# Unit stores on ScalarE's queue, tiles prepared earlier, transfers in quarters, and VectorE instead of GpSimd for the low parts of the turned tiles

## What is computed

```python
x = x + tanh(g_xattn) * cross_attention(layernorm(x), ctx)   # 16 heads, 128 keys per sequence; there are no text keys
x = x + tanh(g_ffn) * ffn(layernorm(x))
# ffn(h): y = square(relu(h @ up)) @ down + (h @ expert) * sum(top2(h @ gate))
#         layernorm(y) * gamma + beta            up 512x2048, down 2048x512, expert 512x512, gate 512x8
```

## Time and profile before

| | |
|---|---|
| median of 3 runs | 1365.26 us |
| the profiled execution | 1362.92 us, span 1361.1 us |
| TensorE busy | 1277.8 us (94%) |
| VectorE, ScalarE, GpSimd busy | 69%, 56%, 43% |
| mean granted TensorE clock | 0.975 |
| transfers | 276.96 MB, mean 203 GB/s |

### The profile page before, as it was taken

How to read it: one execution, slowest core, us unless ns; L and a number is a source line. 1 busy time by engine, 2 the same in 40 slices (tenths; PEclk the granted TensorE clock), 3 DMA queues, 4 the chain that set the end, 5 groups by cost and what they waited for, 6 DMA issues and landing times.

```text
span 1361.1 us, 26319 instructions
## 1 busy us (share of the span) xinstructions
PE 1277.8 (94%) x9154; PEld 1093.8 (80%) x9154; DVE 943.1 (69%) x1568; ACT 755.8 (56%) x2012; POOL 591.3 (43%) x720
## 2 busy tenths in 40 slices
PE   7999999999899999999999999899999899999993
PEld 5887777777777778788899888799888789887993
DVE  6777777777766876665598665697664896366676
ACT  5877777777666757656455343454343543444440
POOL 3766666666655996463034322043311233111033
PEclk9999999999899999999999999899999999999997
DMA  6588888988878864659675687675677664564861
GB/s 226 140 211 222 220 221 222 231 221 213 218 200 196 205 153 115 228 220 237 233 238 177 225 234 221 202 227 176 239 227 223 220 188 165 193 221 153 230 184 62
DMA packets 335460, 276.96 MB, mean 203 GB/s; under 512 B 233852, under 2 KB 248316, under 8 KB 330239
## 3 DMA queue, kind: packets, MB, share of 16 engines
q1 hardware_dynamic: 297600, 165.79, 45.1%
q10 hardware_dynamic: 37758, 109.85, 24.6%
HBM read 198.79 MB, written 76.81 MB: 202 GB/s over the span
## 4 chain that ended last, share of the span: by engine, by line
PE 49%; DVE 16%; DMA 11%; SPq 7%; issue 6%; POOL 5%; ACT 3%; DVEq 0%; POOLq 0%; ACTq 0%
PE wide L79 15%; PE wide L80 14%; PE wide L81 14%; DMA kd_scratch<-kf 6%; SPq L1649 4%; DVE wo_lo L2006 4%; DMA k_dealt<-kd_scratch 3%; PE wide L418 2%; DMA out_x<-fxy 2%; ACT prob L817 1%; PE wide L406 1%; DVE S L1990 1%; POOL fxy L1447 1%; POOL prob L988 1%; PE wide L1728 1%
## 5 line engine op out<-in xcount | busy, mean ns | idle before, releaser
L817 ACT ACTIVATE prob<-wide,nmx 128x128 f32<-128x128 f32 x512 | 180.7, 396 | 6.0 <-DVE nmx L626 5.9
L988 POOL TENSOR_TENSOR prob<-prob,rr 128x512 f32<-128x512 f32 x128 | 136.1, 1075 | 103.9 <-DVE rr L634 103.9
L79 PE MATMUL wide<-eight,wo_hi 128*128 128x256 f32 x480 | 138.0, 288 | 12.5 <-DVE wo_lo L2006 8.3
L1820 ACT ACTIVATE hid<-wide 128x512 f32<-128x512 f32 x96 | 57.4, 599 | 156.6 <-PE wide L81 156.6
L80 PE MATMUL wide<-eight,wo_hi 128*128 128x256 f32 x480 | 136.4, 284 | 0.0
L81 PE MATMUL wide<-eight,wo_lo 128*128 128x256 f32 x480 | 136.3, 284 | 0.0
L2006 DVE TENSOR_TENSOR wo_lo<-hid,wo_hi 128x512 fp32r<-128x512 f32 x120 | 94.6, 810 | 43.6 <-ACT wo_hi L1820 43.6
L817 ACT ACTIVATION_READ_ACCUMULATOR prob<-wide,nmx 128x1 f32 x512 | 121.1, 236 | 0.0
L1820 ACT ACTIVATE wo_hi<-hid 128x512 fp32r<-128x512 f32 x120 | 74.4, 631 | 79.2 <-PE wide L81 79.2
L79 PE MATMUL wide<-wq_hi,eight 128*128 128x512 f32 x192 | 82.9, 432 | 27.1 <-DVE eight L565 27.1
L79 PEld LDWEIGHTS wide<-eight,wo_hi 128*128 128x128 f32 x480 | 92.8, 193 | 16.3 <-issue 9.4
(11 more groups left out here) (308 smaller groups left out, 3971.0 us busy)
## 6 DMA issues: line engine op xcount, KB each, us to landing
eight<-down_scratch ACTq DMA_DIRECT2D x32, 1024.0 KB, 8.0
wk_hi<-down_scratch ACTq DMA_DIRECT2D x12, 1024.0 KB, 7.8
wk_lo<-down_scratch ACTq DMA_DIRECT2D x12, 1024.0 KB, 7.5
wk_hi<-up_scratch ACTq DMA_DIRECT2D x12, 1024.0 KB, 6.8
eight<-up_scratch ACTq DMA_DIRECT2D x12, 1024.0 KB, 5.8
wk_lo<-up_scratch ACTq DMA_DIRECT2D x12, 768.0 KB, 5.6
eight<-up_scratch ACTq DMA_DIRECT2D x12, 768.0 KB, 7.0
xin<-in_x SPq DMA_DIRECT2D x32, 256.0 KB, 3.4
```

What stands on the lines that cost most here:

```text
L79: eng.matmul(dst, ah, bh, start=first and k == 0, stop=False, skip_group_check=onto)
L817: i = act.activation(prob[par][:, g, h * P:(h + 1) * P], cols(bank[g], h), ACT.Exp, bias=nmx[:, n:n + 1], scale=1.0, accum_out=rs[:, n:n + 1])
L988: pool.tensor_tensor(p, p, r, ALU.mult).then_inc(po_p, 1)
L1820: return act.activation(dst, src, ACT.Copy)
```

## The change

Attention: the unit stores are issued by ScalarE, in two parts, the raw one at the top of a slot, the sums after the slot's exponentials; the eight tiles are loaded one per slot from slot 19, with statistics one slot and normalisation two slots later, the latter on VectorE. Feed-forward: residual loads and output stores go in quarters of 32 rows, `weigh` waits for its own tile's store alone, the last group's stores are shared by SP and ScalarE; `lo_T` moves to VectorE; the order of the partial products is 0, 1, 4, 3, 5, 2, 6, with `sum_4` at later steps and written into `hid[q][:, 2]`; in groups 1 and 2 the statistics of the next tiles come at q 0 and 1 and the layer norm of y at q 4 to 7; in the last group VectorE adds the epsilon to the variance.

```diff
-                    if ff.third_of(s, par) is not None:
-                        ff.unit_store(sp, ff.third_of(s, par))           # in SP's slot
+                    if ff.third_of(s, par) is not None:
+                        ff.unit_store_raw(act, ff.third_of(s, par))      # top of ScalarE's slot
+                    if ff.third_of(s, par) is not None:
+                        ff.unit_store_sums(act, ff.third_of(s, par))     # after exps(s, par, 2) and hi_xT(n + 1)
+    def unit_store_raw(act, uu):
+        at_least(act, ql, uu + 2)
+        for part, src in enumerate((t_hi, t_lo)):
...
+                dst = down_dram[uu][0:3, :, part * H:(part + 1) * H].rearrange("o p n -> p o n")
+                act.dma_start(dst, src[:, 0:3 * H].rearrange("p (o n) -> p o n", n=H)).then_inc(st_q, DMA)
+    def unit_store_sums(act, uu):
+        at_least(act, qd, uu + 2)
...
+                dst = down_dram[uu][3:7, :, part * H:(part + 1) * H].rearrange("o p n -> p o n")
+                act.dma_start(dst, src[:, 3 * H:7 * H].rearrange("p (o n) -> p o n", n=H)).then_inc(st_qs, DMA)
+            TILE_LOADED, TILE_STATS, TILE_DONE, PAIR_SUMS = NB - 13, NB - 12, NB - 11, NB - 6
-                    if ff_pair(s) is not None:
-                        ff.stats(dve, 0, ff_pair(s))
-                        ff.stats(dve, 0, ff_pair(s) + GB)
+                    if ff_turn(s, TILE_DONE, ff.TILES) is not None:
+                        ff.normalise(dve, 0, ff_turn(s, TILE_DONE, ff.TILES))
+                    if ff_turn(s, TILE_STATS, ff.TILES) is not None:
+                        ff.stats(dve, 0, ff_turn(s, TILE_STATS, ff.TILES))
-                            ff.normalise(pool, 0, tile)
-    D_SEQ = (0, 3, 4, 2, 5, 1, 6)
+    D_SEQ = (0, 1, 4, 3, 5, 2, 6)
-    TURN_AT = (9, 10, 12, 13, 14, 15, 16, 17)
-    SUMS_AT = (28, 30, 32, 34)
-    HI_AT = (11, 12, 14, 15, 16, 17, 18, 20, 31, 33, 35, 37, 39, 41, 43, 45)
+    TURN_AT = (9, 11, 12, 14, 15, 17, 18, 20)
+    SUM4_AT = (24, 26, 28, 29, 31, 32, 33, 35)
+    SUMS_AT = (36, 39, 41, 44)
+    HI_AT = (11, 13, 14, 16, 17, 19, 20, 22, 38, 41, 43, 46, 47, 48, 49, 50)
+    Y_AT = {4: (0, 1), 5: (2, 3), 6: (4, 5), 7: (6, 7)}
+    def STATS_AT(g):
+        return 1 if g == 0 else 0
-        eng.dma_start(ff.dealt_rows(out[g * GB + i]), y[i]).then_inc(ff.st_o[i % HB], DMA)
+        for src, dst in ff.quarters(y[i], out[g * GB + i]):
+            eng.dma_start(dst, src).then_inc(ff.st_o[i], DMA)
+    def store_half(eng, i, half):                      # last group: half 0 by SP, half 1 by ScalarE
+        eng.wait_ge(ff.dv_o, GB * LAST + i + 1)
+        for src, dst in ff.quarters(y[i], out[LAST * GB + i])[2 * half:2 * half + 2]:
+            eng.dma_start(dst, src).then_inc(ff.st_o[i], DMA)
-            sp.dma_start(res(g, i), ff.dealt_rows(x2_dram[g * GB + i])).then_inc(ff.ld_r[i % HB], DMA)
+            for dst, src in ff.quarters(res(g, i), x2_dram[g * GB + i]):
+                sp.dma_start(dst, src).then_inc(ff.ld_r[i % HB], DMA)
+        def later_group(g):
+            more = g < LAST
+            if more:
+                load_x(g + 1)
+            for i in range(HB):
+                load_res(g - 1, i)
+            if more:
+                for tile in range(GB - 1):
+                    deal(g + 1, tile)
+            for i in range(HB):
+                store_out(sp, g - 1, i)
+                load_res(g - 1, i + HB)
+                if more and i == 1:
+                    deal(g + 1, GB - 1)
+            for i in range(HB, GB):
+                store_out(sp, g - 1, i)
-            at_least(act, ff.st_o[j % HB], 2 * g * DMA)
+            at_least(act, ff.st_o[j], g * KT * DMA)
-                for tile in {1: range(HB), 2: range(HB, GB)}.get(q, ()):
+                for tile in {STATS_AT(g): range(HB), STATS_AT(g) + 1: range(HB, GB)}.get(q, ()):
                     ff.stats(dve, g + 1, tile)
+                if g < LAST and k - 1 in HI_AT:
+                    ff.lo_T(dve, g + 1, HI_AT.index(k - 1))
+        def variance_last(i):
+            dve.wait_ge(ff.dv_ys, 2 * (GB * LAST + i) + 2)
+            dve.tensor_scalar(ff.yvar[:, i:i + 1], ff.ymv[:, i, 1:2], EPS_LN, None, ALU.add).then_inc(ff.fcst, 1)
-            if g < LAST:
-                for i in range(NT):
-                    ff.lo_T(pool, g + 1, i)
```

More of the change, by code:

```diff
@@ L164, in has, with ff_turn @@
                 return not isinstance(b, int) or 0 <= b < NB
-            def ff_pair(b, after=0):
-                jj = b - (NB - 8) - after if isinstance(b, int) else -1
-                return jj if 0 <= jj < GB else None
+            def ff_turn(b, first, order):
+                n = b - first if isinstance(b, int) else -1
+                return order[n] if 0 <= n < len(order) else None
+            TILE_LOADED, TILE_STATS, TILE_DONE, PAIR_SUMS = NB - 13, NB - 12, NB - 11, NB - 6
             def is_slot(b, n):
@@ L1041, in slot @@
                         inv_std(s + 3)
[L1042 to L1045 removed]
+                    if ff_turn(s, TILE_STATS, ff.TILES) is not None:
+                        ff.inv_std(pool, 0, ff_turn(s, TILE_STATS, ff.TILES))
                     if ff.first_of(s, par) is not None:
@@ L1158, in units_stored, with none_stored @@
     def units_stored(uu):
-        return uu * DMA + (max(uu - 2 * NQ, 0) * DMA if isinstance(uu, int) else 0)
+        return DMA + uu * DMA + (max(uu - 2 * NQ, 0) * DMA if isinstance(uu, int) else 0)
+    def none_stored(sp):
+        sp.sem_inc(st_q, DMA)
+        sp.sem_inc(st_qs, DMA)
     def is_up(uu):
@@ L1206, in unit_parts @@
     def unit_parts(uu, a):
[L1207 to L1211, removed]
+        both = raw[:, 0:D] if is_up(uu) else raw.rearrange("p (n m) -> p n m", n=2)[:, :, 0:H]
+        two = a[:, 0:2 * H] if is_up(uu) else a[:, 0:2 * H].rearrange("p (n m) -> p n m", n=2)
+        return [(two, both), (a[:, 2 * H:3 * H], raw[:, 3 * H:4 * H]),
                 (a[:, 3 * H:5 * H], unit_sum[:, 0:2 * H]), (a[:, 5 * H:7 * H], unit_sum[:, 2 * H:4 * H])]
@@ L1685, in group @@
                         ff.piece_load(sp, q + 5)
-                if g > 0 and q in (2, 5):
-                    for i in range(2 * (q // 5), 2 * (q // 5) + 2):
-                        store_out(sp, g - 1, i)
-                        load_res(g - 1, i + HB)
-                if more and q in (4, 5):
-                    for tile in range(HB * (q - 4), HB * (q - 3)):
-                        deal(g + 1, tile)
+                if q in (4, 5):
+                    for tile in range(HB * (q - 4), HB * (q - 3)):
+                        deal(1, tile)
@@ L1693, in group @@
+        for g in range(NG8):
             if g == 0:
[L1694 to L1699 removed]
+                first_group()
+            else:
+                later_group(g)
+            if g < LAST:
                 for i in range(GB):
                     fetch(g + 1, i)
[L1702 to L1705 removed]
@@ L1707, in _ @@
-        for g in range(NG8):
-            group(g)
-        for i in (0, 1, 2, 3, 4, 6):
-            store_out(sp, LAST, i)
-        for n in range(HB):
-            sp.wait_ge(ff.st_o[n], 2 * NG8 * DMA)
+        sp.wait_ge(ff.pe_E, GB * NG8)
+        for i in range(GB):
+            for dst, src in ff.quarters(res(LAST, i), x2_dram[LAST * GB + i]):
+                sp.dma_start(dst, src).then_inc(ff.ld_r[i % HB], DMA)
+        for i in range(GB):
+            store_half(sp, i, 0)
+        for n in range(GB):
+            sp.wait_ge(ff.st_o[n], NG8 * KT * DMA)
@@ L1785, in down_part @@
             return mm3(pe, bank[m % 2 * HB + j][:, 0:H], [(hi[:, cols], lo[:, cols])], [(w[:, 0:H], w[:, H:D])],
-                       first=q == 0 and m in (0, 1, 5), last=q == NQ - 1, onto=m in (2, 3, 4, 6))
+                       first=q == 0 and m in (0, 1, 3), last=q == NQ - 1, onto=m in (2, 4, 5, 6))
         def last_product(g):
```

193 lines of the change are left out of this document (98 added, 95 removed).

## The result

The kernel after takes 1296.71 us (median of 4 runs, 1294.78 to 1298.07), the kernel before 1365.93 beside it: a ratio of 0.949, 95% interval 0.9475 to 0.9509. The forecast was 1305, with a range of 1283 to 1324. The profiled execution has a span of 1294.6 us, where the prediction's sum gave 1301.4.

A forecast was written before the change was run, and what follows sets the result against it. TensorE, busy 94% of the span, bounds the kernel, with its standstills and half-clock stretches; 1361.1 - 34.7 - 7.5 - 14.7 - 10.7 + 13.9 - 6.0 = 1301.4 of span, forecast 1305 us, range 1283 to 1324.

The forecast's parts named there:

- Part 1: Attention's 20 slots with unit stores: taking the stores off SP's list gains 34.7 of the 44.7 us lost.
- Part 2: Attention slots 24 to 28: one tile per slot and normalisation on VectorE gain 7.5 of 8.5 us lost.
- part 3: Expert products of groups 1 and 2 (7.4 and 5.7 us), group 2's first partial product (1.5): 14.7 us gained.
- part 4: Down phases of three groups: lo_T on VectorE, with the steps spread, gains 10.7 us.
- part 5: Start of groups 1 and 2: statistics at q 0 wait for loads ahead of TensorE's adds, losing 13.9 us.
- part 6: The end: last stores in quarters over two queues, a gain of 6 us, bounds 3 and 7.
- The allowance of 1 us per pair: Attention's unit slots: 1 us taken as still lost per pair of slots, with the transfer engines' share at 0.96.
- Rival B: Unit slots: transfer engines bind, a pair stays at 32.5 to 33 us, 22.4 gained; 1317, up to 1326; chance 0.19.
- rival A: Starts of groups 1 and 2: no TensorE standstill at q 0, so 1291 us; chance 0.24.
- The factor for the clock: Up phases of groups 1 and 2: TensorE's 9.9 us standstill multiplied by 1.4, making 13.9.
- these cancel: Last group: low parts gain 1.1 us, eight variances on VectorE cost 0.2 each, inverse root 0.5 sooner, netting nothing.
- Rivals C and D: C: VectorE overflows in down phases, lo_T 1.15 us, 1331, chance 0.06; D: ScalarE's queue blocks at its issues, 1373, 0.03.

## Why the prediction was right

Stage by stage, from the two profiles (after minus before; the predicted column adds up to the prediction's sum):

| | predicted | measured |
|---|---|---|
| attention, to the first expert product (parts 1, 2) | -42.2 | -47.6 |
| expert products (part 3 without the partial product) | -13.2 | -15.4 |
| down phases, groups 0 to 2 (part 4, and 1.5 of part 3) | -12.2 | -12.3 |
| down phase, group 3 | 0 | -2.5 |
| up phases, groups 1 and 2 (part 5) | +13.9 | +16.65 |
| the end (part 6) | -6.0 | -5.3 |
| span | -59.7 | -66.5 |

Some of the closeness is luck: four stages gained 10.2 us more than was put down and two gained 3.5 less, so that the sum is off by 6.8.

**Part 1** was right in mechanism. 38.9 us came where 34.7 was put down. The allowance of 1 us per pair, for a share near full, failed: after, the engines' share is 0.96, and slots 4 to 17 still run at 15.1. What is left over 302.0 is 5.8 us, 5.5 of them in slots 18 to 22: 3.2 in slots 21 and 22, where tile work meets unit work, and 2.3 in slots 18 to 20, where the cause is open. The prediction gave two reasons, another queue and another place, and only the second counts. Rival B, which put half of part 1 at stake, fell: its pairs of 32.5 to 33 us were at 30.2 in slots 4 to 17, though slot 18 waits for transfers.

**Part 2**: 8.5 for 7.5 in slots 24 to 28, but the 1 us left for slot 21 was too little: slots 21 and 22 cost 3.2. The term that was off is "I take 0.9" for the normalisation: it takes 0.52 us when it begins first and 1.53 or 1.42 when GpSimd's add does, and where it meets unit work it is the second.

**Part 3** was right in its sum and didn't ask which of its two halves does the work; the runs say the quarters. Group 3's share, left out, was 1.4 us (24.91 to 23.47).

**Part 4** was right (12.3 with the partial product) and, as it said, needs the step numbers as much as the move. VectorE is busy 65.1 us per down phase, where 68 was worked out. What it left out is that the step numbers also free the last group, which has no `lo_T`: its down phase is 2.5 us shorter (84.74 to 82.24), and 3.0 come back with the old numbers.

**Part 5** was right, the gap came where it was said, and rival A fell. Its term was too small: TensorE stood idle for 7.62 + 5.31 = 12.9 us, not 9.9, since the last of these statistics began 16.1 and 13.8 us into the group instead of 14.0 and 12.4 before, the starts that the prediction went by; the kernels above show that this idle time varies from 9.4 to 12.9 us between kernels that differ elsewhere. The factor for the clock was 16.65 / 12.93 = 1.29, not 1.4.

**Part 6**: 5.3 for 6.0, and the parts of it were otherwise. The stores gave 6.6 us: from VectorE's last step to the end it is 3.3 us instead of 9.9. But "these cancel" was wrong. TensorE's last product comes 2.5 us earlier in the group, and VectorE, which closes the last group, doesn't follow by as much: its last step ends 11.2 us behind that product instead of 9.8.

Rivals C and D fell: `lo_T` takes 0.65 to 0.68 us, and ScalarE's issues of the unit stores mostly take 0.33 to 0.46 and never more than 1.13 (below).

## What to carry to other kernels

Where bulk transfers and a latency-bound chain share the engines, look for the quiet stretch of the chain and put the bulk there, in pieces that fit; try it on the same queue first. An instruction that waits for a load doesn't belong ahead of work that another engine waits for, however idle its own engine is. And look at the outermost dimension of each transfer before tuning the waits on it: 4 instead of 32 cost 29 us in the groups here and 9 at the end.

## What the runs showed of the hardware

A share of the transfer engines near full need not cost time. Slots 4 to 17 of the kernel after ran at 15.1 us with a share of 0.98 and TensorE busy throughout:

```profile
90.66:302.45 211.79, 211.79 (x1793) 175.42 (x1792) 179.57 (x309) 172.67 (x646) 161.88 (x211) 1.00 0.98 251
```

How near to full this holds isn't settled: slot 18, with 1.02, lost 0.8 us and had waits for dealt reads in it. SP's issue of `x_dealt` in one of slots 4 to 17, and ScalarE's of a unit store, from their timelines in the kernel after:

```profile
227.95 0.65 SPq L328 DMA_DIRECT2D x_dealt<-xd_scratch  x1
```

```profile
235.47 0.38 ACTq L1257 DMA_DIRECT2D down_scratch<-hid  x1
```

VectorE and GpSimd don't share evenly: the normalisation that began just behind GpSimd's add ended only after it (1.53 us), the one that began ahead of it was not slowed (0.52). The Trainium skill, in "SBUF — State Buffer", section "SBUF: two separate sides", calls the port pair that the two share an exclusive lock: the operation that starts first has it for the whole instruction. The two pairs of rows agree. The add of 1.28 us cost VectorE 1.01 us here, and one late residual add is enough to make TensorE wait: in the kernel with later statistics, GpSimd's, VectorE's and TensorE's timelines of group 2's down phase:

```profile
1037.30 1.81 POOL L2198 TENSOR_TENSOR sums<-sums,beta 128x512 f32<-128x512 f32 x1 [1.10 <-DMA sums<-x_scratch]
```

```profile
1037.88 2.38 DVE L2056 TENSOR_TENSOR wo_lo<-S,wo_hi 128x512 fp32r<-128x512 f32 x2
...
1039.71 0.39 PE L79 MATMUL wide<-wk_lo,wo_hi 128*128 128x256 f32 x1 [0.60 <-DVE wo_lo L2056]
```
